# Stage ends without POOL's drain, and row buffers zeroed ahead instead of tails written at a stage's end, in a two-layer attention and mixture-of-experts kernel

## What is computed

```python
# kind 0: two of 8 experts per token, C = 2*T/E = 1024 rows kept per expert, the rest dropped
loc1 = jnp.cumsum(mask1, axis=0) - mask1
loc2 = jnp.cumsum(mask2, axis=0) - mask2 + jnp.sum(mask1, axis=0, keepdims=True)
keep1, keep2 = loc1_s < C, loc2_s < C
disp = zeros((E*C, D)).at[f1].add(tokens*keep1).at[f2].add(tokens*keep2)
h = gelu(einsum('ecd,edf->ecf', disp, w_gate))          # F = 512
eo = einsum('ecf,efd->ecd', h, w_down)
out = g1*keep1*eo[f1] + g2*keep2*eo[f2]
# kind 1: two of 8 experts per token, nothing dropped, hidden width 256, a gated silu
```

## Time and profile before

| | |
|---|---|
| median of three runs | 2072.04 us |
| the profiled execution | 2082.38 us, span 2080.5 us |
| PE busy | 1543.0 us, 74% |
| VectorE (DVE) busy | 1178.1 us, 57% |
| ACT busy | 720.2 us, 35% |
| POOL busy | 940.2 us, 45% |
| DMA | 134.91 MB, mean 65 GB/s |
| HBM written | 52.91 MB |

### The profile page before, as it was taken

The page is one execution under the profiler, slowest core; times in us unless marked ns, Lnnn a source line. Parts: engine busy times, 40 slices in busy tenths (PEclk is TensorE's granted clock), DMA queues, the critical chain, the costliest instruction groups (busy, mean ns, idle before and its releaser), DMA issues. The chain is left out here.

```text
span 2080.5 us, 34781 instructions
## 1 busy us (share of the span) xinstructions
PE 1543.0 (74%) x10592; PEld 938.6 (45%) x10592; DVE 1178.1 (57%) x4262; ACT 720.2 (35%) x1339; POOL 940.2 (45%) x1276
## 2 busy tenths in 40 slices
PE   1329938999999998399233992598878788993990
PEld 1219923444444444299222881233333333433880
DVE  3622245566666664122594554777778778843555
ACT  1102213455555553022001330354445445631330
POOL 2745524233443432155474773634454536422771
PEclk9999965999999999599555995587888879965995
DMA  6152210000000000522223882000000000004884
GB/s 219 44 117 66 72 45 16 6 22 16 15 20 10 11 11 13 105 72 69 75 73 97 245 240 67 12 6 16 16 15 14 16 5 11 12 11 106 238 238 130
DMA packets 93868, 134.91 MB, mean 65 GB/s; under 512 B 14784, under 2 KB 72512, under 8 KB 93760
## 3 DMA queue, kind: packets, MB, share of 16 engines
q1 hardware_dynamic: 62768, 88.27, 15.5%
q0 software_dynamic: 17408, 35.82, 5.1%
q10 hardware_dynamic: 13584, 9.48, 1.9%
HBM read 80.61 MB, written 52.91 MB: 64 GB/s over the span
## 5 line engine op out<-in xcount | busy, mean ns | idle before, releaser
L1345 ACT ACTIVATE a_PT<-a_psE 128x512 f32<-128x512 f32 (+1 forms) x512 | 278.0, 543 | 446.0 <-PE a_psE L1509 444.5
L1054 DVE TENSOR_REDUCE a_mx<-a_psS 128x2 f32<-128x512 f32 (+1 forms) x512 | 312.5, 619 | 145.3 <-PE a_psS L1475 144.5
L1532 PE MATMUL a_psV<-a_PT,a_vx 128*32 128x256 f32 (+1 forms) x2048 | 321.8, 397 | 3.0 <-ACT a_PT L1345 0.6
L1475 PE MATMUL a_psS<-a_KT,a_QT 54*128 54x256 bf16 (+1 forms) x1024 | 196.4, 282 | 66.8 <-DVE a_mx L1054 65.5
L1509 PE MATMUL a_psE<-a_QM,a_KT 56*128 56x256 bf16 (+1 forms) x1024 | 199.8, 278 | 1.6 <-issue 0.8
L1907 POOL DMA_INDIRECT slots_y<-e_y,e_ids x160 | 155.3, 970 | 46.6 <-issue 24.4
L1837 PE MATMUL e_psH<-e_rowsT,e_w 128*128 128x256 f32 x640 | 160.3, 395 | 6.4 <-DMA e_w<-in_pack 4.7
L1475 PEld LDWEIGHTS a_psS<-a_KT,a_QT 54*128 54x128 bf16 x1024 | 56.7, 96 | 200.7 <-DVE a_mx L1054 103.5
L1754 POOL DMA_INDIRECT slots_y<-e_y,e_ids x128 | 124.2, 971 | 48.7 <-POOL e_ids L1752 29.2
L1532 PEld LDWEIGHTS a_psV<-a_PT,a_vx 128*32 128x32 f32 x2048 | 77.0, 112 | 118.2 <-issue 82.8
L1837 PEld LDWEIGHTS e_psH<-e_rowsT,e_w 128*128 128x128 f32 x640 | 118.7, 196 | 25.0 <-issue 6.0
(11 more groups left out here) (329 smaller groups left out, 3117.1 us busy)
## 6 DMA issues: line engine op xcount, KB each, us to landing
e_w<-in_pack SPq DMA_DIRECT2D x80, 450.0 KB
e_rows<-slots_x SPq DMA_DIRECT2D x80, 129.0 KB, 2.6
e_rows<-spans_x SPq DMA_DIRECT2D x64, 129.0 KB
a_got<-slots_y SPq DMA_DIRECT2D x32, 256.0 KB
t_got<-slots_y SPq DMA_DIRECT2D x32, 256.0 KB
slots_y<-e_y,e_ids POOLq DMA_INDIRECT x288, 2.2
spans_x<-tail ACTq DMA_DIRECT2D x8, 516.0 KB, 13.4
spans_x<-tail SPq DMA_DIRECT2D x8, 516.0 KB, 17.1
```

Source lines behind the costliest of these rows:

```text
L1054: nc.vector.tensor_reduce(mx[u][:, t, 4 * g + r:4 * g + r + 3:2], psS[c % 2][:, :, 0:cols], AX, ALU.max).then_inc(s_max, 1)
L1345: nc.scalar.activation(PT[:, c % 4, :, q0:SEQ], psE[c % 2][:, :, q0:SEQ], ACT.Exp).then_inc(s_e, 1)
L1475: last = nc.tensor.matmul(psS[c % 2][:, hh, 0:cols], QT[u][64 * r:64 * r + MAXR, k, t * P:(t + 1) * P], KT[u][64 * r:64 * r + MAXR, k, 0:c ...
L1532: last = nc.tensor.matmul(psV[g // 2][32 * quad:32 * quad + 32, g % 2, q0:SEQ], vx[u][:, kt, head, :], PT[:, c % 4, hh, q0:SEQ], start=(kt ...
```

## The change

It has five parts.

1. The blocks end without POOL's drain, and the second barrier of a stage's end is by semaphores only.
2. `spans_x` is zeroed in setup (per expert the 1024 rows from the meeting point up), by SP, and once for both uses. The zeros over the results go from ACT's queue to SP's, behind the weights.
3. `slots_x` is zeroed in e0 by ACT: one region of 4352 rows ahead of its activation of tile 0, 3, 6, ... 21, the spare rows ahead of that of tile 24. POOL waits for the clears ahead of the first scatter of a stage.
4. Tails are gone, and with them the counts' trip to SP and ACT. An empty row is known by count instead: `filled` holds how many rows an expert (or a tile) has, `rank` a row's place, and a mask made at the start of each expert stage gives empty rows their `pad_ids` by max.
5. VectorE's tile table in t1 and a1 gets three operations more and one less, and its reduction runs over 4 x 320 elements instead of 3 x 320.

```diff
     def clear():
         nc.clear_and_free_semaphores(held)
-        nc.all_engine_barrier()
+        nc.all_engine_barrier(sem_only=True)
...
+def clean(eng, keep, dram, first, rows, sem):
+
+    q = rows // ROWS
+    eng.dma_start(dram[first:first + rows, :].rearrange("(p q s) d -> p q (s d)", p=P, q=q),
+                  keep.tail[:, :, :].rearrange("p s d -> p (s d)").unsqueeze(1)
+                  .to_broadcast([P, q, ROWS // P * (D + 1)])).then_inc(sem, 16)
...
-        block = ctx.enter_context(nc.Block())
+        block = ctx.enter_context(nc.Block(no_gpsimd_drain=True))
 
         @block.sync
         def _(sp):
             sp.dma_start(f[:, :], consts).then_inc(s_load, 16)
             sp.dma_start(keep.x[:, :, :], x_in.rearrange("(n p) d -> p n d", p=P)).then_inc(s_load, 16)
+            sp.wait_ge(s_tail, 1)
+            for e in range(E):
+                clean(sp, keep, spans, e * SPAN + TOKENS, CAP, keep.s_spans_clean)
             sp.dma_start(keep.kept_w[:, :, :], kept.rearrange("e p n -> p e n")).then_inc(keep.s_kept_w, 16)
+            n = TOKENS * TOPK // P
+            sp.dma_start(results[0:TOKENS * TOPK, :].rearrange("(p n) d -> p n d", p=P),
+                         keep.tail[:, 0:1, 0:D].to_broadcast([P, n, D])).then_inc(keep.s_no_result, 16)
             sp.wait_ge(s_load, 32)
-
-        @block.scalar
-        def _(act):
-            act.wait_ge(s_tail, 1)
-            n = TOKENS * TOPK // P
-            act.dma_start(results[0:TOKENS * TOPK, :].rearrange("(p n) d -> p n d", p=P),
-                          keep.tail[:, 0:1, 0:D].to_broadcast([P, n, D])).then_inc(keep.s_no_result, 16)
...
     def pool_scatter(self, pool, chain, b, w):
+        if is_first(b):
+            pool.wait_ge(*self.clean)
         wait(pool, self.s_rows, b + 1)
...
-        if self.capacity:
-            self.close_spans(act, range(1, E, 2))
-        else:
-            self.clear_tails(act, range(E // 2, E), False)
-
...
-        link(nc.vector.tensor_tensor(cnt[:, 4, :], keep.meet[:, 0, :], self.R[:, 0, :], ALU.add))
-        nc.vector.tensor_copy(keep.spans[:, :, :], cnt[:, 3:5, :]).then_inc(self.s_counts, 1)
...
+        nc.vector.tensor_tensor(keep.filled[:, 0:E], cnt[:, 0, :], cnt[:, 2, :], ALU.add)
+        nc.vector.tensor_copy(keep.spans[:, :], cnt[:, 3, :])
...
-        nc.vector.tensor_copy(keep.counts[:, :], cnt[:, 0, :]).then_inc(self.s_counts, 1)
...
+        link(nc.vector.scalar_tensor_tensor(
+            out=cnt[:, 5, :], in0=cnt[:, 3, :], scalar=float(ROWS), in1=cnt[:, 0, :],
+            op0=ALU.mult, op1=ALU.add))
...
         nc.vector.tensor_tensor(tt[:, 0, :, :], tt[:, 2, :, :], per_e(cnt[:, 4, :]), ALU.mult)
+        nc.vector.tensor_tensor(tt[:, 3, :, :], tt[:, 2, :, :], per_e(cnt[:, 5, :]), ALU.mult)
...
-        link(nc.vector.tensor_reduce(tr[:, 0:3, :], tt[:, :, :, :], AX, ALU.add))
+        link(nc.vector.tensor_reduce(tr[:, 0:4, :], tt[:, :, :, :], AX, ALU.add))
...
-            if route:
-                route.sp_end(sp)
...
-                r = sp.value_load(keep.spans[0:1, 0, e:e + 1], min_val=0, max_val=SPAN_ROWS - CAP)
-                sp.wait_ge(keep.s_ends[e], 16 * use)
+                r = sp.value_load(keep.spans[0:1, e:e + 1], min_val=0, max_val=SPAN_ROWS - CAP)
...
             for j in range(COUNT):
+                if to_clean is not None and j % 3 == 0 and j // 3 < E:
+                    clean(act, keep, to_clean, j // 3 * REGION, REGION, keep.s_slots_clean)
+                if to_clean is not None and j == 3 * E:
+                    clean(act, keep, to_clean, SPARE, ROWS, keep.s_slots_clean)
                 act.wait_ge(s_H, j + 1)
...
+            link = Chain(dve, s_dve)
+            for e in range(E):
+                link.later(nc.vector.tensor_scalar(empty[:, e, :, :], keep.rank[:, :, :], keep.filled[:, e:e + 1],
+                                                   None, ALU.is_ge))
+            link.sync()
+            link(nc.vector.tensor_tensor(
+                over[:, :, :, :].rearrange("p e t s -> p e (t s)"), empty[:, :, :, :].rearrange("p e t s -> p e (t s)"),
+                keep.pad_ids[:, :, :].rearrange("p t s -> p (t s)").unsqueeze(1).to_broadcast([P, E, U * S]), ALU.mult))
...
                     nc.vector.tensor_tensor(ids0[:, s % U, :], rows[:, s % U, :, D].bitcast(I32),
-                                            keep.pad_ids[:, s % U, :], ALU.min)
+                                            over[:, s // KEPT_TILES, s % KEPT_TILES, :], ALU.max)
...
-        kept_stage(nc, keep, "e0", 1, spans_x, slots_y)
+        kept_stage(nc, keep, "e0", spans_x, slots_y, slots_x)
```

More of the change, by code:

```diff
@@ L103, in __init__ @@
         self.s_no_result = nc.alloc_semaphore("results_zeroed")
-        self.s_ends = [nc.alloc_semaphore(f"ends{e}") for e in range(E)]
+        self.s_spans_clean = nc.alloc_semaphore("spans_clean")
+        self.s_slots_clean = nc.alloc_semaphore("slots_clean")
 def stage_semaphores(nc, ctx, tag):
@@ L317, in __init__ @@
         self.held = held
+        self.clean = (keep.s_spans_clean, 16 * E) if capacity else (keep.s_slots_clean, 16 * (E + 1))
         self.nc, self.keep, self.slots, self.has_bias, self.capacity = nc, keep, slots, has_bias, capacity
@@ L354, in __init__ @@
         self.s_exp = sem("gap_exp")
-        self.s_counts = sem("counts")
-        self.s_zero = sem("tails")
     def sp_load(self, sp, router):
@@ L606, in tile_table @@
         link(nc.vector.scalar_tensor_tensor(
[L607 removed]
+            out=tr[:, 6, :], in0=keep.iota_tiles[:, :], scalar=float(ROWS), in1=tr[:, 2, :],
             op0=ALU.mult, op1=ALU.mult))
[L609 to L610 removed]
+        link(nc.vector.tensor_tensor(tr[:, 4, :], tr[:, 6, :], tr[:, 0, :], ALU.add))
@@ L611, in tile_table @@
+        link(nc.vector.tensor_tensor(tr[:, 6, :], tr[:, 4, :], tr[:, 5, :], ALU.add))
         nc.vector.tensor_copy(keep.table[:, :, 0], tr[:, 1, :])
-        nc.vector.tensor_copy(keep.table[:, :, 1], tr[:, 3, :])
-    def clear_tails(self, eng, experts, spare):
-        eng.wait_ge(self.s_counts, 1)
-        for e in experts:
-            c = eng.value_load(self.keep.counts[0:1, e:e + 1], min_val=0, max_val=TOKENS)
-            eng.dma_start(self.slots[bass.ds(c + e * REGION, ROWS), :].rearrange("(p s) d -> p (s d)", p=P),
-                          self.keep.tail[:, :, :].rearrange("p s d -> p (s d)")).then_inc(self.s_zero, 16)
-        if spare:
-            eng.dma_start(self.slots[SPARE:SPARE + ROWS, :].rearrange("(p s) d -> p (s d)", p=P),
-                          self.keep.tail[:, :, :].rearrange("p s d -> p (s d)")).then_inc(self.s_zero, 16)
-        eng.wait_ge(self.s_zero, 16 * (E + 1))
@@ L626, in sp_end @@
-    def sp_end(self, sp):
-        if self.capacity:
-            self.close_spans(sp, range(0, E, 2))
-        else:
-            self.clear_tails(sp, range(E // 2), True)
+        nc.vector.tensor_copy(keep.table[:, :, 1], tr[:, 6, :])
 def looped_steps(eng, first, lo, hi, last, step, per=2):
@@ L1629, in _, with kept_stage @@
             looped_steps(pe, -3, 4, 12, 18, step)
[L1632 removed]
+def kept_stage(nc, keep, tag, slots_in, slots_out, to_clean=None):
     HID = UP // P
@@ L1653, in kept_stage @@
         y = sb("y", [P, U, S, D], F32)
+        empty = sb("empty", [P, E, KEPT_TILES, S], F32)
+        over = sb("over", [P, E, KEPT_TILES, S], I32)
         ids0 = sb("ids0", [P, U, S], I32)
@@ L1786, in expert_stage @@
         y = sb("y", [P, U, S, D], F32)
+        empty = sb("empty", [P, MOE_TILES, S], F32)
+        over = sb("over", [P, MOE_TILES, S], I32)
         ids0 = sb("ids0", [P, U, S], I32)
@@ L1888, in step @@
                     dve.wait_ge(s_Y, s + 1)
-                    nc.vector.tensor_tensor(ids0[:, u, :], rows[:, u, :, D].bitcast(I32), keep.pad_ids[:, u, :],
-                                            ALU.min)
+                    nc.vector.tensor_tensor(ids0[:, u, :].unsqueeze(1), rows[:, u, :, D].bitcast(I32).unsqueeze(1),
+                                            over[:, bass.ds(s, 1), :], ALU.max)
                     src = psY[u % 2][:, 0:S * D].rearrange("p (s d) -> p s d", s=S)
@@ L1894, in step @@
                         ALU.add).then_inc(s_y, 1)
+            link = Chain(dve, s_dve)
+            link(nc.vector.tensor_tensor(
+                empty[:, :, :], keep.rank[:, 0, :].unsqueeze(1).to_broadcast([P, MOE_TILES, S]),
+                keep.filled[:, :].unsqueeze(2).to_broadcast([P, MOE_TILES, S]), ALU.is_ge))
+            link(nc.vector.tensor_tensor(
+                over[:, :, :].rearrange("p (i u) s -> p i (u s)", u=U), empty[:, :, :].rearrange("p (i u) s -> p i (u s)", u=U),
+                keep.pad_ids[:, :, :].rearrange("p u s -> p (u s)").unsqueeze(1)
+                .to_broadcast([P, MOE_TILES // U, U * S]), ALU.mult))
             looped_steps(dve, -2, 4, 36, 39, step, U)
```

49 lines of the change are left out of this document (21 added, 28 removed).

## The result

The changed kernel took 2084.1 us in the median of 17 runs, the kernel before 2064.2 us on the same chip: ratio 1.0097, 95% interval 1.0066 to 1.0128, so 14 to 26 us slower. 2071 us, one microsecond less than before, was forecast; the range of 2028 to 2104 held the time. The one profiled execution (span 2084.2 us, the one before 2080.5) shows only 3.7 us of it, mainly since a1 was granted a mean clock of 0.84 there instead of 0.80 (575.6 us long against 595.0). So the stages are compared one by one.

The account below looks back on a forecast made before the run. TensorE was taken to bound e0, and POOL's drains and waits for scatters the boundaries behind scatters. -69.1 + 22.5 (start) + 45 (e0) = -1.6 us on the median 2072.0 gave 2071 us, range 2028 to 2104.

Parts of the forecast that it names:

- What goes: Stage boundaries: drains 45.0 us, tails 22.4 us and e1's first row load 1.7 us are gained, 69.1 us in all.
- What is added at the start: Setup to t0: t_wr stands last on SP's queue, so TensorE starts 22.5 us later; bounds 14 and 27.
- the bound of 27: Start of t0: 27 us later if VectorE's start again waits 10 us under the load until the queue is empty.
- t_wr lands near 52.5: Start of t0: by summed transfer rates the small load lands near 52.5 us, and TensorE starts 22.5 us later.
- What is added in e0: Stage e0: ACT's clears make row loads late, 37 us, and lower the clock, 8 us; together 45 us, bounds nothing and 90.
- I take half of it: Row loads in e0: half of a small transfer's 8.5 us wait, 4.2 us, so each load meeting the stream is 1.8 us late.
- 13.3 us hold 2.5 of them: Clears in e0: 13.3 us of DMA work per period meets 2.5 late loads, 4.6 us per region, eight times 37 us.
- The clock: Stage e0: a lower granted clock for TensorE adds 1 us per region, 8 us in all.
- Rival one: Stage e0: loads keep their slack as the stream only takes turns; e0 costs 0 to 24 us, 2026 to 2050; chance 0.35.
- Rival two: Stage e0: loads much later or clock low for the stage, from 67 us on, 2093 to 2116; chance 0.25.
- Rival three: Stage boundaries: the drain's work comes back in a later scatter or at the end; with half returned 2093; chance 0.05.
- The case that came: The forecast itself: e0 costs 24 to 67 us, total 2050 to 2093 us; chance 0.35.

Follow-up runs that it names:

- d1_no_drain: The kernel before, with only POOL's drain left out at every stage's end and in the barrier behind it; 2023.8 us against 2048.2, ratio 0.9859.
- w1_router_first: The changed kernel, with the 8 KB of router weights loaded in setup ahead of the span clears; 2040.8 us, ratio to before 0.9947.
- r1_rows8: The changed kernel, with eight row buffers instead of four in e0, clears unchanged; 2026.7 us, ratio to before 0.9882.
- p1_thirds: The changed kernel, with each of e0's eight region clears issued in three pieces, one per tile; 2081.9 us against 2110.9, ratio 0.9843.
- al_aligned: The changed kernel, real clears moved to a0, aligned 1024-byte writes to an unread tensor in their place in e0; 2086.2 us, ratio to before 0.9888.

## Why the prediction was wrong

**What goes: right.** 69.1 us forecast, 67.8 in the trace, boundary by boundary. Two sizes inside were off and cancelled: the drain was worth less than its length where tails were in flight (3.7 and 2.4), the tails more; t1's tails were to give 2.6 and gave 0.4 to 1.5 where single runs show them, and nothing in the changed kernel (17.3 us from t1 to e2, 17.2 in d1_no_drain, which has the tails).

**What is added at the start: wrong by 5.8 us (22.5, measured 28.3, above the bound of 27).** "t_wr lands near 52.5: TensorE starts" there. The rates held within a few us (t_wr handed over at 52.7, landed by 55.5), but the step from t_wr to TensorE was left out: VectorE waits for t_wr before its statistics, and TensorE is 2.8 us behind VectorE. The earlier trace rows had it: 27.20 and 29.98, VectorE idle for 10.46 before. I read that wait as an effect of load and priced it as a bound, instead of asking which semaphore stands between the two instructions in the code. w1_router_first shows that it was t_wr.

**What is added in e0: the mechanism right, its size not: 45 forecast, 57.3 measured.** The failed steps are "I take half of it" and "13.3 us hold 2.5 of them". The delay is not half of another transfer's 8.5 us and does not fall on each load alike: the load behind a clear waits for some 60 of the clear's pieces on each engine, and takes 8.9 us (r1_rows8) instead of 2.1; with a third of the write ahead of it there is nearly no wait (p1_thirds). One load per clear makes TensorE wait, 5.1 us, and the next one comes in right behind it. Seven times 5.1 + 2.1 of clock (14.6 / 7) are the 50.1; the forecast had eight times 4.6 + 1, near it for reasons of another kind. w1_router_first has seven times 4.0 + 1.8. Rows of before could have given a wait of this size, as an estimate: if a load waited for the whole clear, the clear's 10.8 us by rate and 2.1 for a landing, less the 2.7 from a tile on ACT to the next row load (165.25 and 167.92 in the timelines of before), less that load's 4.5 us of time, would be 5.7.
And one load was not counted: e0's own first, behind the first clear, 7.2 us. It is on the path whole.

**The clock**: forecast 8 us, measured 14.6 (12.8 in w1_router_first). It followed the waits and did not stay low: with the waits gone (r1_rows8) it was 1.00.

**The rules.** The Trainium skill (*DMA: Bandwidth & Descriptors*, "Queues, rings and completion order") says that an engine takes turns between queues packet by packet, and that such a packet holds typically 9 to 17 descriptors and at most 64. The prediction counted a load's 8 pieces per engine as 8 packets and let the stream move 8 pieces for them; that is not what the page says. With 9 to 17 pieces the load would wait an estimated 0.7 to 1.3 us (pieces of 1032 bytes on 16 engines at 208 GB/s), still inside its 2.4 us. The traces show some 60 pieces per engine, far above the typical packet and below the limit; so they speak against the count in the prediction and not against turns. Of the page's other rule that the prediction weighed, on stalled writes to another core, the late loads are what it would lead to, but no run shows that writes stalled.

**The rivals.** Rival one (the loads keep their slack) had rested on that count. It got 0.35 and should have had less: the earlier trace rows had already spoken. Rival two (67 us and more) did not come as priced, but its working was nearer than the forecast's: with the whole 8.5 us it made a load 6 us late and e0 66 us longer, where 5.1 and 57.3 were measured. Rival three (the drain's work comes back) did not come.

**The whole.** -67.8 + 28.3 + 57.3 = +17.8 instead of -1.6. Of the 19.4 us, 12.3 are e0's, 5.8 the start's, 1.3 missing gains. The case that came was one of the two given 0.35, and its own range (2050 to 2093) holds the time; the sum fell on the wrong side since both added terms were taken too low, the one for a consumer passed over, the other for a halving that no row supported. With e0 as w1_router_first had it (41.3 + 6.9) the forecast's 45 would be 3 us short. So e0's 12.3 are in part one execution's; the start's shortfall is in every run that has t_wr last (TensorE's first work at 56.7 to 58.3, 4.2 to 5.8 more than forecast).

## What to carry to other kernels

Work that is moved beneath another stage is hidden only if each transfer of that stage has more time to spare than it waits behind one write of the moved work: cut the write (thirds made 50 us into 3.5), deepen the buffers (2.6), or take a stage whose loads are issued long ahead (nothing). At a moved queue ask for each small load who consumes it, all engines included, and put it ahead of the bulk: 8 KB at the end of 12.6 MB cost 28 us, ahead of them 0.7. And end-of-stage costs that overlap each other (drain, tails in flight, the first load behind them) are worth less singly than together.

## What the runs showed of the hardware

- A row load of 8 pieces per engine on SP's queue, issued 2.7 us behind a write of 136 pieces per engine on ACT's, moved its first piece 4.3 to 6.0 us after its issue instead of 1.0; some 60 pieces per engine of the write went ahead in the difference (953, 941 and 986 on 16 engines, in the changed kernel, r1_rows8 and al_aligned).
- Writes of 1032 bytes that begin anywhere and of 1024 that begin at multiples of 1024, as many of each: 18.5 us per period of e0 against 12.4 to 15, and 230 to 250 GB/s against 290 while they are under way.
- A full queue shows at the issuer: SP needed 25.3 us for one DMA of 8 KB behind 12.6 MB, and 10.7 to 16.5 us for eight clears whose issue takes ACT 0.54 each in e0. In setup this also delays the stage's end (VectorE enters t0 at 27.51), since SP cannot leave.
- POOL's drain behind scatters takes 5.3 to 6.7 us though POOL has waited for them, 34 ns where there are none (t2), and without it (d1_no_drain) no stage became longer by more than it differs between two executions of before (a0: 540.5 us against 532.2 and 541.1).
